# The thirty VectorE products of a turn, grouped in eight operations in place of thirteen

## The reference, cut to what matters

```python
B, M, D = (2048, 32, 16)          # batch, fields, embedding width
x0 = e                            # e: (2048, 32, 16), gathered from tbl_0 .. tbl_31 by ids
xk = x0
for W in (W0, W1, W2):            # each layer has 64 outputs
    xk = relu(einsum('bmd,bhd,mhk->bkd', x0, xk, W))
    outs.append(sum(xk, axis=2))
z = concatenate(outs, axis=1)     # (2048, 192)
h = concatenate([z, dense_ctx], axis=1)
h = maximum(h @ W_top1 + b_top1, 0.0)
h = maximum(h @ W_top2 + b_top2, 0.0)
y = h @ W_top3
```

## Time and profile before

| quantity | value |
|---|---|
| time, median of 3 runs | 1216.67 us (1216.64 to 1218.73) |
| time of the profiled execution | 1227.56 us |
| span of the profiled execution | 1225.8 us |
| mean granted TensorE clock | 0.986 |
| TensorE busy | 1122.7 us, 92% of the span |
| VectorE busy | 1116.5 us, 91% |
| ScalarE busy | 731.8 us, 60% |
| GpSimd busy | 923.2 us, 75% |

### The profile page before, as it was taken

The page is one execution under the profiler, slowest core; times in us unless marked ns, Lnnn a source line. Parts: engine busy times, 40 slices in busy tenths (PEclk is TensorE's granted clock), DMA queues, the critical chain, the costliest instruction groups (busy, mean ns, idle before and its releaser), DMA issues.

```text
span 1225.8 us, 14619 instructions
## 1 busy us (share of the span) xinstructions
PE 1122.7 (92%) x5312; PEld 395.7 (32%) x5312; DVE 1116.5 (91%) x519; ACT 731.8 (60%) x1361; POOL 923.2 (75%) x642
## 2 busy tenths in 40 slices
PE   0267999999999999999999999999999999999997
PEld 0022233333343333334333333333333333333334
DVE  0158999999999999999999999999999999999994
ACT  0036656765675666666666766576576657657652
POOL 6767888788887878788787878878787887875400
PEclk9878999999999999999999999999999999999998
DMA  5967877657688676768877566787767677776200
GB/s 117 188 126 157 166 152 148 140 120 150 133 167 166 137 147 125 146 128 159 167 149 148 119 144 131 151 165 152 152 130 141 130 146 158 164 153 131 53 1 1
DMA packets 76088, 167.25 MB, mean 136 GB/s; under 512 B 21648, under 2 KB 38944, under 8 KB 76016
## 3 DMA queue, kind: packets, MB, share of 16 engines
q1 hardware_dynamic: 59088, 161.95, 63.1%
q0 software_dynamic: 16384, 4.23, 3.7%
q10 hardware_dynamic: 544, 0.14, 0.1%
HBM read 157.86 MB, written 8.40 MB: 136 GB/s over the span
## 4 chain that ended last, share of the span: by engine, by line
PE 78%; DVE 11%; issue 8%; ACT 2%; another core or an unknown queue 1%; ACTq 0%; DVEq 0%
PE acc L578 72%; DVE p_dve L504 11%; PE acc L648 3%; PE acc L636 1%; PE acc L638 1%; ACT xb L305 1%; PE acc L656 1%; DVE z L531 1%; ACT x_s L314 0%; ACT xa L296 0%; ACT L323 0%; ACT out_l L389 0%; ACT h L418 0%; ACT p_l L323 0%
## 5 line engine op out<-in xcount | busy, mean ns | idle before, releaser
L578 PE MATMUL acc<-p_dve,w_s 128*64 128x512 f32 x3840 | 864.0, 597 | 51.9 <-DVE p_dve L504 48.8
L244 POOL DMA_INDIRECT x_rows<-in_table,ids_s x512 | 488.8, 955 | 145.9 <-issue 132.7
L504 DVE TENSOR_TENSOR p_dve<-spread,xb 128x3072 f32<-128x3072 f32 (+2 forms) x224 | 567.2, 2586 | 16.4 <-PE acc L578 16.4
L504 DVE TENSOR_TENSOR p_dve<-spread,xa 128x2048 f32<-128x2048 f32 (+1 forms) x192 | 495.6, 2637 | 35.2 <-issue 31.1
L578 PEld LDWEIGHTS acc<-p_dve,w_s 128*64 128x64 f32 x3840 | 267.5, 137 | 602.9 <-issue 493.2
L305 ACT ACTIVATE xb<-acc 32x512 f32<-32x512 f32 x512 | 288.8, 564 | 84.5 <-DVE p_dve L504 78.1
L256 POOL TENSOR_TENSOR p_l<-spread,q_tile 128x2048 f32<-128x2048 f32 x62 | 281.8, 4570 | 11.5 <-DMA q_tile<-x_of_steps 8.3
L296 ACT ACTIVATE xa<-acc 64x512 f32<-64x512 f32 x256 | 145.9, 570 | 205.2 <-PE acc L578 110.7
L267 POOL TENSOR_TENSOR p_pool<-spread,x_s 128x1024 f32<-128x1024 f32 x64 | 152.4, 2381 | 121.9 <-PE acc L578 66.3
L578 PE MATMUL acc<-p_l,w_s 128*64 128x512 f32 (+1 forms) x640 | 150.4, 606 | 45.4 <-issue 45.4
L314 ACT ACTIVATE x_s<-acc 64x512 f32<-64x512 f32 x256 | 151.2, 591 | 3.5
(11 more groups left out here) (18 smaller groups left out, 159.1 us busy)
## 6 DMA issues: line engine op xcount, KB each, us to landing
spread<-x_of_steps SPq DMA_DIRECT2D x256, 512.0 KB
q_tile<-x_of_steps SPq DMA_DIRECT2D x128, 128.0 KB
x_rows<-in_table,ids_s POOLq DMA_INDIRECT x512
x_of_steps<-x_rows SPq DMA_DIRECT2D x64, 128.0 KB
w_s<-in_w SPq DMA_DIRECT2D x2, 512.0 KB
wt<-in_w_top SPq DMA_DIRECT2D x1, 512.0 KB
z_all<-in_dense_t ACTq DMA_DIRECT2D x16, 8.0 KB
wt<-in_w_top SPq DMA_DIRECT2D x1, 256.0 KB
```

Source lines behind the costliest of these rows:

```text
L244: nc.gpsimd.indirect_dma_start(out=x_rows[:, s % 2, i * DIM:(i + 1) * DIM], out_offset=None, in_=table, in_offset=bass.IndirectOffsetOnAxi ...
L504: nc.vector.tensor_tensor(p_dve[:, to:to + n, :], spread[:, s % 3, tile:tile + n, :], over(x[:], n), ALU.mult).then_inc(dve_made, n)
L578: last = nc.tensor.matmul(acc[b * K:(b + 1) * K, :], w, prod[:, b * BLK:(b + 1) * BLK], start=start, stop=stop)
```

## The change

Only the grouping changes. A pair is (first chunk, number of chunks).

```diff
-GROUPS_L1 = [(0, 3), (3, 2), (5, 2), (8, 3), (11, 3), (14, 2)]
-GROUPS_L2 = [(0, 2), (2, 3), (5, 2), (8, 3), (11, 1), (12, 2), (14, 2)]
+GROUPS_L1 = [(0, 5), (5, 2), (8, 4), (12, 4)]
+GROUPS_L2 = [(0, 4), (4, 3), (8, 3), (11, 5)]
...
             for s in range(STEPS):
-                for c, n in GROUPS_L1:
+                for c, n in GROUPS_L1 if s > 0 else GROUPS_L2:
...
-            for c, n in GROUPS_L2:
+            for c, n in GROUPS_L1:
                 if c == NT:
                     sums(STEPS - 2, 1)
                     sums(STEPS - 2, 2)
-                if c == CL - 2:
+                if c == GROUPS_L1[-1][0]:
                     sums(STEPS - 1, 1)
                 layer2(STEPS - 1, c, n)
```

## The result

| | before | changed |
|---|---|---|
| median | 1217.17 us (4 runs, 1216.64 to 1218.73) | 1295.82 us (4 runs, 1293.76 to 1297.49) |
| ratio | | 1.0643, 95% interval 1.0621 to 1.0665 |
| span of the profiled execution | 1225.8 us | 1292.6 us |
| VectorE busy, operations | 1116.5 us, 519 | 1106.7 us, 359 |

The changed kernel is 78.7 us slower; the forecast was 1295. The spans differ by only 66.8, because the profiled execution before began its first layer product at 67.84 us and the one after at 55.87. From that product to the end it is 1157.96 against 1236.73, 78.8 more.

A forecast was written before the change was run, and what follows sets the result against it. The ring of ten chunks between VectorE and TensorE, nearly equally loaded, was taken as the bound. Middle turns +73.4, first turns +1.8 and +0.4, last +3 gave +78.6 on 1216.67, so 1295 us; range 1280 to 1312.

The forecast's parts named there:

- the line of two forms: VectorE's product durations, 3.35 us for three chunks and 2.28 for two, extended to operations of four and five chunks.
- Plain turn: Turn without MLP work, counted from chunk 4's start on TensorE to the next chunk 4: 37.11 us, before 34.61.
- MLP turn: Turn in which TensorE also does MLP parts, counted from chunk 4 to the next chunk 4: 38.83 us.
- From chunk 4 of turn 1 to that of turn 30: 14 MLP turns and 15 plain ones: before 1026.9 us, after 1100.3, so +73.4.
- The first turns: Turn 0's five ends later and delays layer 0, +1.8 us; turn 1 adds the four ahead of layer 0, +0.4.
- The last turn: The (11, 5) wait and late (0, 5) occur once more without a layer 0: about +3 us.
- A cover of 1.9: GpSimd's layer-0 products, after the later load_a, end at 686.6, TensorE reaches layer 0 at 688.5; nothing counted.
- A: VectorE is saturated, so its removed operations show in full: 10 us less, 1207 us; chance 0.04.
- A': The gain from fewer operations and the new waits cancel: 1214 to 1219 us; chance 0.02.
- B: The waits come but are counted too high, since TensorE's stalls swallow each other: 1258 us; chance 0.06.
- C: Loads become late through load_a: 1382 us at worst, 1310 to 1340 if only plain turns are hit; chance 0.07.
- D: TensorE's new stalls each bring a stretch at half clock, 116 us more, 1411 us; chance 0.03.

The follow-up runs named there:

- experiment 1: The changed kernel with the five of layer 2, (11, 5), cut into (11, 3) and (14, 2): 1263.11 us.
- experiment 2: The changed kernel with layer 0 of the next step placed after chunk 4 of layer 2, not after chunk 3: 1263.76 us.
- experiment 3: The kernel before, with load_a waiting for all 15 products of layer 2 and no group changed: 1217.66 us.
- experiment 9: The kernel before with one operation fewer a turn, (11, 1) and (12, 2) of layer 2 joined to (11, 3): 1216.14 us.
- experiment 4: The changed kernel with the old groups (3, 2, 2, 3, 3, 2) for layer 1 and its new ones for layer 2: 1304.5 us.

## Why the prediction was right

**The forecast of 1295 against 1295.82**, by its steps:

- A five was taken from the line of two forms as 5.49 long and 5.40 to the next. Measured 5.49, and 5.41 (686.39 to 691.80). Right.
- The five of layer 2 waits for chunk 4 behind layer 0, once a turn, longer after MLP work. Measured in every turn, 2.84 and 4.54; experiments 1 and 2 took the wait away from either side, for 32 us each.
- Plain turn 37.11, MLP turn 38.83. Measured 37.22 and 38.92. The 0.1 lies at one hand-over: chunk 0 of layer 2 started 4.55 after its group (709.84 to 714.39), not 4.46. It is 0.14 after the operation's end there, where the row of before that I used had 0.04.
- From chunk 4 of turn 1 to that of turn 30, +73.4. From the waits released by it: before 1027.6 (my 1026.9), after 1103.3, so +75.6. Too small by 2.2, which is 29 times those 0.1 less the 0.7 on the side of before.
- The first turns, +2.2. In the two profiles of before and after it was +2.1 for my 1.8 in turn 0; from the first product to the release in turn 1 57.87 before and 60.28 after, +2.4 for my 2.2. But this was the beginning of one execution, not of the kernel: its first product came at 67.84, and in the thirteen other profiles of this document it came at 52.88 to 55.87. Experiment 3 has the groups and the time of before, and its edit acts on the loads from step 3 on. Its VectorE and TensorE in turn 0, and chunk 4 of turn 1:

```profile
53.05 7.75 DVE L504 TENSOR_TENSOR p_dve<-spread,xa 128x3072 f32<-128x3072 f32 x3 [6.45 <-issue]
...
74.59 1.94 PE L578 MATMUL acc<-p_l,w_s 128*64 128x512 f32 x8 [1.91 <-POOL p_l L256]
78.96 2.94 PE L578 MATMUL acc<-p_l,w_s 128*64 128x512 f32 x12 [2.42 <-POOL p_l L256]
...
115.39 6.23 PE L578 MATMUL acc<-p_dve,w_s 128*64 128x512 f32 x28
```

  Here layer 0 of turn 0 waits for GpSimd with the old groups, 1.91 and 2.42 us, and these waits cover what the large groups cost there: chunk 4 of turn 1 starts at 115.39, after the change at 114.95. So against an ordinary execution the first turns cost -0.4, and the term of +2.2 was too large by 2.6.
- The last turn, +3, with bounds for the ends together of 0 and 9. From the release in turn 30 to the last MLP tile's first matmul 61.35 and 64.64: +3.3. The size is right and the reason given for it is not: neither wait occurs once more (VectorE does not wait in turn 31, whose layer 2 has no layer 0 in it). Of the 3.3, 2.5 have come about by the head of the last turn, since three chunks more, 3.2 us, stand behind the release of chunk 4 in turn 30, less the overhead and a wait that are gone, and 0.8 in the last turn, which ends with a four. The MLP tile itself, at the end where nothing overlaps, ran in the profile of before at a granted clock of 0.69 and after at 1.00, which took 2.6 off the difference of the two profiles; in experiment 3 it ran at 1.00 too.
- The sum. Against experiment 3 the three parts are -0.4, +76.4 and +3.3, together +79.3, the difference of the two profiled executions (1215.08 and 1294.35). The forecast had +2.2, +73.4 and +3. The middle was 3.0 too small and the first turns 2.6 too large; they cancelled, so that the closeness of the total is in part luck. The mechanism held, and the period of a pair was right to 0.2 us.
- The prediction says that chunks 11 to 13 needed two to four used chunks before. By the formula of the ring (11, 1) needs one and (12, 2) three. All of them are ahead of layer 0, as it says, so nothing in the sum changes.
- A cover of 1.9 for GpSimd's layer-0 products, counted at nothing. Only 0.3 was left (717.56 against 717.85), since q_tile took 16.5 and not 14.7. Experiment 3 shows that the late load alone costs nothing with the old groups too. Right in the sum, thinner than I said.

**The rivals.** A (saturated, so overhead in full): VectorE's busy time did fall by 9.8, but it came back as waits; experiment 9 shows on a single operation how that goes. The Trainium skill, page "Perfetto Trace Analysis", section "Optimizing Scalar/DVE Operations", has that larger operations can raise throughput if the engine is saturated; VectorE was busy for 69.42 of 70.88 us and the larger ones cost 79. The 60 ns that the prediction took from there is the Trainium skill's figure for operands in SBUF; the products here read one of theirs from PSUM, so the 0.06 to 0.07 of this trace is no test of it. A' and B fell with the pair at 76.14. C fell with experiments 1 to 3; in the whole trace of the changed kernel TensorE waits for GpSimd's layer-0 products once, for 0.9 us. D was not met at stalls of 1.4, and was met in experiment 4 at 2.5.

## What to carry to other kernels

Where a buffer of k places joins a producer and a consumer of nearly equal load, an operation that fills n places cannot start before the last of them is free, and hands nothing over until it ends: price a larger group by what stands between it and the place that it now needs (here a whole layer 0), not by the overhead that it saves. Then look for the group at which the consumer starves and make that one small; here two smaller ones at the head of layer 2 were worth 18 us, while five operations fewer a turn cost 79. The sum over one turn, carried through both engines in the unit prices of one trace, came within 0.4% of the measured time for twelve of the thirteen kernels here, and some 0.8% short where a stall let the clock fall. For the experiments only the pair of turns was worked out in this way, and the time was counted from a kernel already measured (experiment 1 writes it out).

## What the runs showed of the hardware

- The duration of VectorE's product of two f32 operands, one in PSUM, is linear from two to five chunks: 2.28, 3.35, 4.42, 5.49 us for 2048 to 5120 columns, and the next operation may start 0.09 before its end.
- TensorE's granted clock fell to 0.50 behind a stall of 2.53 us in seven of fifteen equal turns and not in the other eight, at the same stall and the same work around it (experiment 4); what decides between the two isn't shown. Stalls of 1.4 us, three a plain turn, never brought it down in the changed kernel (1.00 from 100 to 1200 us).
- ScalarE's wait for a load grew from 94 to 168 us over the kernel without any change of the time (experiment 3).
